# A routed expert layer whose block table is built in two parts

## The reference

```python
x = L0_attn_x
xn = _layernorm(x, axis=-1)
x = x + _L0_attn_ref(xn, ...) + _L0_ffn_ref(xn, L0_ffn_Wg, L0_ffn_Wu, L0_ffn_Wd)
xn = _layernorm(x, axis=-1)
x = x + _L1_attn_ref(xn, ...) + _L1_ffn_ref(xn, ...)

# _L0_ffn_ref: 8 experts, every token goes through all of them
h = silu(x @ wg) * (x @ wu); acc = acc + h @ wd          # 128 -> 512 -> 128

# _L1_attn_ref: a stack of 4 layers, each:
x = x + _attention(_layernorm(x, ln1w, ln1b), aw, ab, pw, pb)   # Hamilton products, spectral filter
x = x + gelu(_layernorm(x, ln2w, ln2b) @ fw + fb) @ mw + mb     # 128 -> 512 -> 128

# _L1_ffn_ref: 8 experts, each token is weighted into its two best ones
bids = sigmoid(x @ conf_w.T + conf_b) * wealth
top_bids, selected_experts = top_k(bids, 2); routing_weights = softmax(top_bids)
output = sum over the two of routing_weight * expert(x)
```

## Time and profile before

| what | us |
|---|---|
| median of 3 runs (1594.21 to 1597.24) | 1597.03 |
| the profiled execution | 1592.25 |
| its span (first to last instruction) | 1590.4 |
| PE busy in the span | 1480.2 |
| DVE busy | 1167.9 |
| ACT busy | 1039.9 |
| POOL busy | 341.8 |

### The profile page before, as it was taken

One profiled execution on the slowest core, in us unless ns is written; L12 is line 12 of the kernel. 1 busy time (PEld: TensorE's weight loads), 2 busy tenths in 40 slices (PEclk: granted clock), 3 DMA queues, 4 the chain that ended last, 5 costly groups with the idle time before them and its releaser, 6 DMA issues.

```text
span 1590.4 us, 20945 instructions
## 1 busy us (share of the span) xinstructions
PE 1480.2 (93%) x6278; PEld 988.1 (62%) x6278; DVE 1167.9 (73%) x1414; ACT 1039.9 (65%) x2503; POOL 341.8 (21%) x251
## 2 busy tenths in 40 slices
PE   6999999999999999999999999999779999999978
PEld 4677657666556655556656655655447767877655
DVE  3434644895689869999459957998979855799495
ACT  7457547657676777767687658577766576667742
POOL 0001203111411230103111401131134432344230
PEclk9999999999999999999999999999889999999989
DMA  6754434334244434344344334351155545554433
GB/s 237 271 193 154 137 116 149 117 116 162 88 138 124 157 102 127 113 153 127 102 139 155 101 95 120 110 148 49 48 163 165 157 126 161 166 158 142 150 109 120
DMA packets 109675, 217.32 MB, mean 137 GB/s; under 512 B 13687, under 2 KB 57420, under 8 KB 108076
## 3 DMA queue, kind: packets, MB, share of 16 engines
q1 hardware_dynamic: 105020, 206.60, 41.5%
q0 software_dynamic: 4544, 9.38, 1.7%
HBM read 168.81 MB, written 39.93 MB: 131 GB/s over the span
## 4 chain that ended last, share of the span: by engine, by line
PE 43%; issue 19%; DVE 15%; ACT 15%; POOL 4%; DMA 3%; SPq 1%; POOLq 0%; ACTq 0%; DVEq 0%
PE bank L1250 6%; PE bank L1416 4%; PE bank L1238 4%; PE bank L1240 4%; PE bank L1239 4%; PE bank L1410 4%; PE bank L1328 3%; ACT ROWS L781 3%; POOL RSTD L945 2%; PE bank L1451 2%; ACT ROWS L794 2%; DVE AM L1003 2%; PE bank L1390 2%; DVE SH L1115 2%; DVE TA L999 2%
## 5 line engine op out<-in xcount | busy, mean ns | idle before, releaser
L945 POOL TENSOR_TENSOR RSTD<-SS,power_half 128x4 f32<-128x4 f32 x96 | 138.1, 1439 | 933.8 <-ACT ROWS L781 933.6
L1238 PE MATMUL bank<-NH,GU 128*128 128x512 f32 x512 | 265.7, 519 | 1.6 <-ACT SH L772 1.2
L1115 DVE TENSOR_TENSOR SH<-SH,bank 128x512 f32<-128x512 f32 x256 | 171.8, 682 | 129.0 <-ACT SH L772 89.2
L1250 PE MATMUL bank<-SH,WD 128*128 128x512 f32 x512 | 262.2, 594 | 0.0
L999 DVE TENSOR_TENSOR TA<-QK 128x2048 f32<-128x2048 f32 x96 | 219.5, 2287 | 1.3
L772 ACT ACTIVATE SH<-bank 128x512 f32<-128x512 f32 x256 | 151.4, 602 | 98.6 <-PE bank L1240 95.9
L781 ACT ACTIVATE ROWS<-bank,root_eps 128x128 f32<-128x128 f32 x384 | 135.5, 368 | 113.1 <-PE bank L1328 113.0
L1240 PE MATMUL bank<-NL,GU 128*128 128x512 f32 x512 | 205.0, 400 | 0.0
L1239 PE MATMUL bank<-NH,GU 128*128 128x512 f32 x512 | 204.0, 398 | 0.0
L1003 DVE TENSOR_TENSOR AM<-AM,TA 128x1024 f32<-128x1024 f32 x128 | 153.0, 1218 | 0.8
L1451 PE MATMUL bank<-XT,GU 128*128 128x256 f32 x624 | 145.5, 379 | 0.5 <-ACT XT L921 0.5
(11 more groups left out here) (205 smaller groups left out, 2576.2 us busy)
## 6 DMA issues: line engine op xcount, KB each, us to landing
GU<-halves SPq DMA_DIRECT2D x112, 512.0 KB
GU<-in_w_gu SPq DMA_DIRECT2D x39, 512.0 KB
xg<-in_c_fill SPq DMA_DIRECT2D x8, 2080.0 KB
WD<-in_w_d SPq DMA_DIRECT2D x128, 128.0 KB
QK<-QK SPq DMA_DIRECT2D x32, 480.0 KB
WD<-in_w_d SPq DMA_DIRECT2D x39, 256.0 KB
halves<-GU SPq DMA_DIRECT2D x8, 1024.0 KB, 8.6
FC<-ready_w SPq DMA_DIRECT2D x32, 256.0 KB
```

Of the source, the lines that this page charges most:

```text
L945: pool.tensor_tensor(RSTD[:], SS[:], (power_one if k[0] == "at" else power_half)[:], ALU.pow).then_inc(power_done, 1)
L1115: dve.tensor_tensor(SH[:, g % 4, :], SH[:, g % 4, :], banks[2 + g % 2][:], ALU.mult).then_inc(h_ready, 1)
L1238: pe.matmul(out, w_hi, x_hi, start=True, stop=False)
L1250: pe.matmul(banks[4][:], WD1[:, slot, :], SH[:, g % 4, :], start=first, stop=last).then_inc(down_done, 1)
```

## The change

1. The table is built in two parts. With seven tiles routed (7168 assignments) and eight experts, at least 21 blocks are full: an expert leaves at most 255 rows over, and (7168 - 8 x 255) / 256 rounds up to 21 (`FIRST`). `table 0` stands after `route (6, 3)` and lists 21 full blocks; `table 1` stands after tile 7's routing and lists the other 18, leaving out what the first took (`TAKEN`).
2. `load_x` of blocks 0 to 20 waits for seven tiles' scatters, not for eight. `load_w` of blocks 0 to 3 waits for the last use of layer 0's buffers: `down_done` (all 256 down matmuls), `ya_ready`, `kv_done`, `q_done`.
3. The buffers are laid out anew. `GU`, `WD`, `XT`, `YS` now lie exactly over `GU1`, `WD1`, `NH`, `NL`; `XR` and the table's arrays lie over `KV`.
4. In the planner the ACT part of a centring is 1.45 instead of 1.0, powers 1.5 instead of 1.4, scales 1.1 instead of 1.0; the urgency constants of most steps are other numbers. The order of every engine is computed anew; each engine has the same steps as before, except one more `table` on DVE.

```diff
+ROUTED = TILES - 1
+FIRST = -(-(2 * ROUTED * TILE - EXPERTS * (BLOCK - 1)) // BLOCK)
...
-            step("power", k, urgency, [(POOL, 1.4)], [("den", key, ACT_)])
-            step("scale", k, urgency, [(ACT_, 1.0)], [("power", k, POOL), ("centre", k, PE)])
+            step("power", k, urgency, [(POOL, 1.5)], [("den", key, ACT_)])
+            step("scale", k, urgency, [(ACT_, 1.1)], [("power", k, POOL), ("centre", k, PE)])
...
-            step("centre", k, urgency, [(PE, 0.9, ("LN",), gives), (ACT_, 1.0)], after)
-            step("power", k, urgency, [(POOL, 1.4)], [("centre", k, ACT_)])
-            step("scale", k, urgency, [(ACT_, 2.0 if kind == "n3" else 1.0, ("YF",) if kind == "n3" else ())], [("power", k, POOL)])
+            step("centre", k, urgency, [(PE, 0.9, ("LN",), gives), (ACT_, 1.45)], after)
+            step("power", k, urgency, [(POOL, 1.5)], [("centre", k, ACT_)])
+            step("scale", k, urgency, [(ACT_, 2.1 if kind == "n3" else 1.1, ("YF",) if kind == "n3" else ())], [("power", k, POOL)])
...
-    NORM3 = (-32.06, -2.73)
+    NORM3 = (-37.1, 32.53)
...
-        step("route", (t, 3), r, [(DVE, 2.5, (), ("6",))], [("route", (t, 2), ACT_), ("route", (t, 2), PE)])
+        step("route", (t, 3), r, [(DVE, 2.5, (), ("6",))], [("route", (t, 2), ACT_), ("route", (t, 2), PE)]
+             + ([("table", 0, DVE)] if t >= ROUTED else []))
...
-    START = (35.92, 58.4)
+    START = (36.84, 38.37)
...
-    step("load_numbers", 0, -500, [(SP, 0.1)], [("route", (TILES - 1, 3), DVE)])
-    step("table", 0, -500, [(DVE, 4.9)], [("load_numbers", 0, SP, 2.5)])
+    step("load_numbers", 0, -500, [(SP, 0.1)], [("kv_sum", BATCHES - 1, PE)])
+    step("table", 0, -500, [(DVE, 5.0)], [("load_numbers", 0, SP, 2.5), ("route", (ROUTED - 1, 3), DVE)])
+    step("table", 1, -500, [(DVE, 5.4)], [("table", 0, DVE), ("route", (TILES - 1, 3), DVE)])
     for g in range(BLOCKS):
         u = LATE + PACE * g
-        step("load_w", g, u - 9, [(SP, 0.8)], [("table", 0, DVE)] + ([("down", g - DEEP, PE)] if g >= DEEP else []))
-        step("load_x", g, u - 3, [(SP, 0.4)], [("table", 0, DVE), ("scatter", (TILES - 1, 7), POOL, 3.0)] + ([("y_store", (g - DEEP, 1), POOL, 2.0)] if g >= DEEP else []))
+        when = int(g >= FIRST)
+        step("load_w", g, u - 9, [(SP, 0.8)], [("table", when, DVE), ("last_down", 0, PE), ("normed", ("at", TILES - 1), DVE)] + ([("down", g - DEEP, PE)] if g >= DEEP else []))
+        step("load_x", g, u - 3, [(SP, 0.4)], [("table", when, DVE), ("scatter", (TILES - 1 if when else ROUTED - 1, 7), POOL, 3.0)] + ([("y_store", (g - DEEP, 1), POOL, 2.0)] if g >= DEEP else []))
         step("turn_in", g, u, [(PE, 0.22, ("4",)), (ACT_, 0.27, (), ("4",), [("gate_up", (g - 2, 1), PE)] if g > 1 else [])],
-             [("load_x", g, SP, 4.0)])
+             [("load_x", g, SP, 4.0), ("add_experts", TILES - 1, DVE)])
...
         GU1 = sb("GU1", [P, SLOTS, 2, 2 * P], F32R)
         WD1 = sb("WD1", [P, SLOTS, P])
+        NH, NL = sb("NH", [P, HALVES, TILE], F32R), sb("NL", [P, HALVES, TILE], F32R)
+
+        KV = sb("KV", [P, HALVES * GROUPS, 2 * P + 2])
+
         raw = sb("raw", [P, 2, CHUNKS, 2 * P])
         AW = 3 * P + 2 * H0
+        AH, AL = sb("AH", [P, AW], F32R), sb("AL", [P, AW], F32R)
         attn_raw = sb("attn_raw", [P, AW])
-        AH, AL = sb("AH", [P, AW], F32R), sb("AL", [P, AW], F32R)
         WDA = sb("WDA", [P, 3, P])
         kv_bias = sb("kv_bias", [P, 2 * P])
         conf = sb("conf", [P, EXPERTS])
         cols = sb("cols", [P, 12])
-        NH, NL = sb("NH", [P, HALVES, TILE], F32R), sb("NL", [P, HALVES, TILE], F32R)
-        KV = sb("KV", [P, HALVES * GROUPS, 2 * P + 2])
         KVS = sb("KVS", [P, P + 2])
...
-        XR = sb("XR", [P, DEEP, 2, P + 2])
         XT = sb("XT", [P, 2, BLOCK])
         YS = sb("YS", [P, 2, 2, P])
-        YL = sb("YL", [P, YSLOTS, 2, GROUPS, P])
+        XR = sb("XR", [P, DEEP, 2, P + 2])
         block_no = sb("block_no", [1, BLOCKS])
         FILL, FULL = sb("FILL", [P, EXPERTS]), sb("FULL", [P, EXPERTS])
         END = [sb(f"END{i}", [P, 2 * EXPERTS]) for i in range(2)]
-        PAST, SKIP = (sb(n, [1, BLOCKS, EXPERTS]) for n in ("PAST", "SKIP"))
-        OWNERF, ROW0F = (sb(n, [1, BLOCKS]) for n in ("OWNERF", "ROW0F"))
+        TAKEN = sb("TAKEN", [P, EXPERTS + 1])
+        PAST, SKIP = (sb(n, [1, FIRST, EXPERTS]) for n in ("PAST", "SKIP"))
+        OWNERF, ROW0F = (sb(n, [1, FIRST]) for n in ("OWNERF", "ROW0F"))
+        YL = sb("YL", [P, YSLOTS, 2, GROUPS, P])
...
-                sp.wait_ge(routed, TILES)
+                sp.wait_ge(kvs_done, BATCHES)
                 sp.dma_start(block_no[:], A["c_block_no"][:, 0:BLOCKS]).then_inc(numbers_loaded, 16)
             elif name == "load_w":
                 i = k % DEEP
-                sp.wait_ge(table_set, 1)
+                sp.wait_ge(table_set, 1 + (k >= FIRST))
...
                 if k >= DEEP:
                     sp.wait_ge(down3_done, k - DEEP + 1)
+                else:
+
+                    sp.wait_ge(down_done, TILES * SPAN)
+                    sp.wait_ge(ya_ready, nth["at", TILES - 1])
+                    sp.wait_ge(kv_done, 2 * TILES)
+                    sp.wait_ge(q_done, TILES)
...
-                sp.wait_ge(scattered, 16 * 2 * NG)
+
+                sp.wait_ge(scattered, 16 * 2 * (ROUTED * GROUPS if k < FIRST else NG))
...
-        def block_table():
-
+        def block_table(last):
+
+
+            some = slice(FIRST, BLOCKS) if last else slice(0, FIRST)
+            count = some.stop - some.start
             dve.wait_ge(numbers_loaded, 16)
-            dve.wait_ge(rank_read, TILES)
-            for e in END:
-                dve.memset(e[:], 0.0)
+            dve.wait_ge(rank_read, TILES if last else ROUTED)
             link(dve.tensor_tensor(FILL[:], BASE[:], OFF[:], ALU.subtract))
-            link(dve.tensor_scalar(FILL[:], FILL[:], 1.0 / BLOCK, (BLOCK - 1.0) / BLOCK - 0.5 + 0.5 / BLOCK, ALU.mult, ALU.add))
+            part = (0.5 if last else -0.5) * (BLOCK - 1.0) / BLOCK
...
+            if last:
+                link(dve.tensor_tensor(FULL[:], FULL[:], TAKEN[:, 0:EXPERTS], ALU.subtract))
+            else:
+                dve.memset(TAKEN[:], 0.0)
+                for e in END:
+                    dve.memset(e[:, 0:EXPERTS], 0.0)
...
+            if last:
+
+                link(dve.tensor_tensor(END[0][:, EXPERTS:], TAKEN[:, 1:], TAKEN[:, 0:EXPERTS], ALU.subtract))
+                link(dve.scalar_tensor_tensor(FILL[:], END[0][:, EXPERTS:], float(BLOCK), FILL[:], ALU.mult, ALU.add))
+            else:
+                link(dve.tensor_scalar(END[0][:], END[1][:], float(FIRST), None, ALU.min))
+                link(dve.tensor_tensor(TAKEN[:, 0:EXPERTS], END[0][:, EXPERTS:], END[0][:, EXPERTS - 1:2 * EXPERTS - 1], ALU.subtract))
...
-            dve.tensor_copy(ROW0[:], ROW0F[:])
-            dve.tensor_scalar(OWNER[:], OWNERF[:], EXPERTS - 1.0, None, ALU.min).then_inc(table_set, 1)
+            link(dve.tensor_tensor(skip, past, FILL[0:1, :].unsqueeze(1).broadcast_to(shape), ALU.mult))
+            link(dve.tensor_reduce(owner, past, AX.X, ALU.add))
+            link(dve.tensor_reduce(row0, skip, AX.X, ALU.add))
+            link(dve.scalar_tensor_tensor(row0, number, float(BLOCK), row0, ALU.mult, ALU.add))
+            if last:
+                link(dve.scalar_tensor_tensor(row0, TAKEN[0:1, 0:1].broadcast_to([1, count]), float(BLOCK), row0, ALU.mult, ALU.add))
+            dve.tensor_copy(ROW0[:, some], row0)
+            dve.tensor_scalar(OWNER[:, some], owner, EXPERTS - 1.0, None, ALU.min).then_inc(table_set, 1)
...
+                pe.wait_ge(ya_ready, nth["at", TILES - 1])
                 pe.wait_ge(xt_copied, k)
```

More of the change, by code:

```diff
@@ L195, in schedule @@
     EARLY = 60.0
-    NORM0 = (-0.91, -55.8)
-    KEYS = (5.25, 9.4)
-    KV_SUM = 14.67
-    QUERY = (15.0, 36.79)
-    ATTN = (-7.21, 18.93)
-    NORM1 = (4.12, 60.26)
-    FFN2 = (67.27, -48.32)
-    NORM2 = (9.93, 112.4)
-    ROUTE = (4.0, 3.97)
-    NORM3 = (-32.06, -2.73)
+    NORM0 = (0.22, -59.59)
+    KEYS = (-0.03, 10.16)
+    KV_SUM = 13.39
+    QUERY = (37.58, 14.61)
+    ATTN = (-6.27, 31.95)
+    NORM1 = (23.92, 60.26)
+    FFN2 = (67.27, -31.99)
+    NORM2 = (9.93, 112.22)
+    ROUTE = (-26.39, 14.62)
+    NORM3 = (-37.1, 32.53)
     for t in range(TILES):
```

17 lines of the change are left out of this document (8 added, 9 removed).

## The result

| | before | after |
|---|---|---|
| median of the runs, us | 1595.62 (1591.78 to 1597.24, 4 runs) | 1557.30 (1555.30 to 1559.53, 4 runs) |
| ratio, 95% interval | | 0.9764 (0.9740 to 0.9787) |
| profiled execution, us | 1592.25 | 1557.16 |
| its span, us | 1590.40 | 1555.3 |

The change saves 38 us between the medians and 35.1 us between the profiled executions. The direction and the closing of the hole were forecast. The gain of 11.8 us ahead of the hole, a third of the whole, was not, and 1557.3 lies under the low end of 1560. Of the 17.5 us between the forecast of 1574.8 and the result, 12.9 are in the span (1568.2 forecast, 1555.3 measured). The other 4.6 are an offset: I set the runs' median 4.8 us above the profiled execution, as it was before, and after the change it is 0.1 above.

A forecast was written before the change was run, and what follows sets the result against it. TensorE (PE), 93% busy, was taken as the bound. The terms -31.9 + 3.5 + 1 + 2.5 + 2 + 1.7 - 1 gave -22.2 us, from 1597.03 to 1574.8 us; range 1560 to 1593.

The forecast's parts named there:

- the hole: The 71.47 us from layer 0's last down matmul to layer 1's first expert matmul: 31.9 us that other matmuls could fill.
- (a): First block weight loads wait for the last down matmul, so PE idles before the first gate matmul: 3.5 us cost.
- (f): One short half-clock stretch remains near the crossing from layer 0's experts to layer 1's blocks: 1.7 us cost.
- (b): Building the block table twice: the first build, before tile 7's experts, costs DVE time, 1 us; the second is hidden.
- (e): The first 1109 us planned anew: 2 us loss, bounded by a gain of 10 and a loss of 12.
- (d): Tile 7's scatters on POOL between block 3's row stores delay later blocks' transposes: 2.5 us cost, 0 to 12 possible.
- tail: Tile 7's last layer starts once tile 6's last products are done; matmuls ahead of it differ by 1.6 us: -1 us.
- my sign: The stretch of 70 us behind the last down matmul over 94% busy, at a clock of 0.97 or more.
- (c): First four x loads stand ahead of layer 0's weight load 121 on SP; 6 us of cover, so 0 cost.
- the 3 to 8 of the forecast: Sign: block transposes wait 3 to 8 us in total for `xg` loads after tile 7's scatters.
- the fuller gain: Rival: the hole closes fully and the new order also waits less before it; -36.7 us, near 1560, chance 0.12.
- Half coming back as new waits: Rival: blocks and layers compete for DVE, layers slip and their latency reappears at PE; -11.7 us, 1585, chance 0.18.

The follow-up runs named there:

- second profile of after: The changed kernel run and profiled again, unchanged: 1558.73 us, ratio 0.9784 to the kernel before.
- the two steps moved: Against the changed kernel, cosines of (7,3) put ahead of (6,3)'s gelus on ACT, and (6,3)'s output addition behind (7,3)'s sixth product on DVE: 1551.54 us, ratio 0.9741.

## Why the prediction was wrong, point by point

| term | forecast | measured as loss at starts |
|---|---|---|
| hole, with (a) and (f) | -31.9 + 3.5 + 1.7 = -26.7 | -29.7 (second profile of after: -28.0) |
| first part, (b) + (e) | +1 + 2 = +3 | **-11.8** |
| middle, (d) | +2.5 | +2.6 |
| tail | -1 | +4.4 (second profile: +2.3) |

- **The hole: right.** By starts it lost 35.5 us, not 31.9, and 5.8 are left where the forecast left 5.2. (a) said that the first gate would stand 6.6 us or more behind the last down; it stands 7.1 behind, with 2.1 us of waits instead of 3.5. The last down came at 1111.1, not 1123, since the part ahead shrank. (f) charged 1.7 for one short half-clock stretch: none in the first profile, one in the second (1.2 us lost in it). PE is 93.6% busy at 1.00 there; my sign was over 94%.
- **(b): as forecast, as far as the runs can tell.** The two halves of the table lie at 1005 to 1009 and at 1169 to 1174 us. The changed kernel's first part loses 1.5 us more than the same numbers without the early table (64.7 against 63.2), with one more group in it.
- **(c): right.** No wait for a weight load stands in the last half tile.
- **(d): the size came, not by the cause I gave.** PE waits 4.0 us for `xg` loads in the 368 us behind the last down, within the 3 to 8 of the forecast, but it waited 5.0 us for them before, and ahead of the blocks' transposes the middle loses 7.6 us where it lost 9.1. What the middle takes back stands ahead of the layers' matmuls (`mproj` 2.1, views 1.2, `freq` 0.6, centrings 0.7 us more) and of gate and up (0.9). That the sum hit 2.5 is luck.
- **(e): the step that failed.** I wrote that no row prices an order, took a loss of 2 because DVE would come nearer to PE, and bounded the gain at 10, a quarter of PE's idle time. The last two are wrong, and the first overlooks a row. Idle time is a poor bound: it fell from 45.3 to 44.0 us, while the loss at starts fell from 76.5 to 64.7 us, 4.2 of it at the low clock, which my bound left out. DVE's load rose, 820 us busy instead of 784, and PE did not suffer. And rows do show what the planner had wrong: the profile of before has a norm with its engines nearly free. In the last layer, on PE, ACT, POOL, ACT and PE:

```profile
1570.84 1.06 PE L1328 MATMUL bank<-centre,Z 128*128 128x128 f32 x8
1571.93 0.37 ACT L781 ACTIVATE ROWS<-bank,root_eps 128x128 f32<-128x128 f32 x1 [10.04 <-PE bank L1328]
1573.22 0.21 ACT L781 ACTIVATION_READ_ACCUMULATOR ROWS<-bank,root_eps 128x1 f32 x1
1573.51 1.01 POOL L945 TENSOR_TENSOR RSTD<-SS,power_half 128x4 f32<-128x4 f32 x1 [29.15 <-ACT ROWS L781]
1574.55 1.14 ACT L794 ACTIVATE ROWS<-bank,RSTD 128x128 f32<-128x128 f32 x4 [1.12 <-POOL RSTD L945]
1575.74 0.66 PE L1334 MATMUL bank<-ident,ROWS 128*128 128x128 f32 x4 [0.28 <-ACT ROWS L794]
```

  ACT holds the squares for 1.50 us (1571.93 to 1573.43), where the planner had 1.0, and the scale for 1.14, where it had 1.0; all 96 such groups of squares in this profile have a median of 1.50. So the planner of before gave ACT 0.6 us too little for each norm that has squares, 72 of the 80 ahead of the last down. The whole way is another matter. From the centring's end on PE (1570.84 + 0.89) to the turn are 4.0 us; the planner counted 1.0 + 1.4 + 1.0 and four hand-overs of 0.2, 4.2 us, and counts 4.85 now. It did not have the way too short on free engines. It took ACT, which all norms share, to be free sooner than it is, and the new number puts 0.45 us more on ACT and 0.45 us more between a centring and its turn at once. No run parts these two.

  The loss by starts says where the gain lies: ahead of the turns it fell from 23.3 to 12.0 us, which is 11.3 of the 11.8 us; 4.2 come from the low clock, and the other matmuls lose 3.7 more. With PE's steps at the lengths of the earlier trace rows the mean distance in PE's order from a centring to its turn rose from 5.0 to 5.5 us. To count turns with little cover says less: 16 of 80 stood less than 4.05 us of PE work behind their centring before and 10 of 82 do now, but 8 of each are `at` norms, whose power waits for `den` and not for the centring, and the kernel with the centring alone set back has 10 of 81 as well. That kernel loses 20 us more than the changed one: 4.5 ahead of turns, 8.9 in half-clock stretches, and the rest ahead of other matmuls. What is shown is that this one number separates the plans, and that most of the changed kernel's gain stands at the turns; how the number acts on the rest stays open.
- **Rivals.** The time that came is that of the fuller gain (-36.7, 0.12), and the reason I gave for it holds: the corrected cost concerns the largest wait. Its other terms did not come: it had (d) at nothing and the tail at -1, and the middle and the tail took back 7.0 us, which the hole and the first part made up for. Against it I had put that the stretches ahead of the hole were at 96% already; that share did not move and the time fell. Half coming back as new waits is what the split does with the old numbers.
- **The tail: sign wrong.** I compared PE's matmuls ahead of the last layer and found 1.6 us of difference. The end is not set by those but by DVE's chain of products, and that chain started late because of one step's place on ACT. The centring of tile 7's last norm A stands 82 us from the end, not 74 to 76. With the two steps moved, the end loses less than before the change.

## What to carry to other kernels

A planner's costs can be held against the trace: for each step, put the time from its first to its last instruction on an engine beside the length that the planner counts, and keep that apart from the latency of the chain, hand-overs included. Bound what a new order can give by the loss at starts, low clock included, not by the idle time, and book each loss under the matmul that started late. A hole on the bounding engine can be lead for the chains beside it; where it is filled, look at what the last chain then waits for, and when a step is moved ahead, follow what was put behind it to its first reader on every engine. A sign that was there before the change (here the waits for `xg`) proves nothing unless it is compared with its value before.
